# The last softmax chunk of the first message pass, twelve pairs, becomes one of eight and one of four

## What is computed

```python
h_src = h_all[edge_type, src]
scores = einsum(h_src, attn_src) + einsum(h_dst, attn_dst)
scores = where(scores > 0, scores, 0.2 * scores)
amax = maximum(segment_max(scores, dst), 0.0)
w = exp(scores - amax[dst])
denom = segment_sum(w, dst) + 1e-12
out = segment_sum(h_src * (w / denom[dst])[..., None], dst)
```

## Time and profile before

| what | us |
|---|---|
| three runs | 2943.80, 2944.15, 2945.18 |
| median | 2944.15 |
| span of the profiled execution | 2937.4 |
| median less span (what lies around it) | 6.75 |
| gathers of the first pass (POOL L1412), 392 of them | 355.7 to 848.4 |
| its first and last weighing (DVE L1643) | 407.3 and 891.8 |
| its last add (DVE L1657) ends | 894.4 |
| DVE, first instruction of the next stage | 895.5 |
| PE busy, DVE busy, ACT busy, POOL busy over the span | 78%, 48%, 36%, 46% |

### The profile page before, as it was taken

One profiled execution on the slowest core, in us unless ns is written; L12 is line 12 of the kernel. 1 busy time (PEld: TensorE's weight loads), 2 busy tenths in 40 slices (PEclk: granted clock), 3 DMA queues, 4 the chain that ended last, 5 costly groups with the idle time before them and its releaser, 6 DMA issues. The chain is left out here.

```text
span 2937.4 us, 42780 instructions
## 1 busy us (share of the span) xinstructions
PE 2285.9 (78%) x11338; PEld 1700.9 (58%) x11338; DVE 1402.4 (48%) x3454; ACT 1054.5 (36%) x2797; POOL 1365.4 (46%) x1426
## 2 busy tenths in 40 slices
PE   3899737767677988999994697876754998874996
PEld 3455324445455877888883465554543777663775
DVE  6665426667666231111115332242248666656677
ACT  2422224545442212332332443265411656441320
POOL 1122277777740051111110577777757777774300
PEclk8999958888878899999997898988775999997998
DMA  6256544444421024666763533343556444445001
GB/s 199 73 175 201 160 114 119 119 119 118 119 67 31 1 73 142 213 210 200 220 202 108 152 106 105 106 137 114 164 156 206 127 136 134 126 120 161 18 1 44
DMA packets 244439, 374.16 MB, mean 127 GB/s; under 512 B 66888, under 2 KB 179860, under 8 KB 244234
## 3 DMA queue, kind: packets, MB, share of 16 engines
q0 software_dynamic: 64624, 179.69, 21.4%
q1 hardware_dynamic: 132718, 140.75, 15.6%
q10 hardware_dynamic: 46892, 51.32, 5.3%
HBM read 301.77 MB, written 69.88 MB: 127 GB/s over the span
## 5 line engine op out<-in xcount | busy, mean ns | idle before, releaser
L2677 POOL DMA_INDIRECT cm_rows<-rows,e_bsrc x392 | 374.1, 954 | 202.0 <-issue 102.4
L1412 POOL DMA_INDIRECT at_rows<-values,e_brow x392 | 373.6, 953 | 139.8 <-issue 86.9
L1138 POOL DMA_INDIRECT store<-rows,e_bsrc x392 | 377.2, 962 | 119.5 <-issue 105.7
L1492 PE MATMUL at_part<-at_msg,store 128*128 128x265 f32 x880 | 272.4, 453 | 89.3 <-DVE at_msg L1643 46.5
L2813 PE MATMUL cm_part<-cm_rows,cm_one 128*128 x880 | 264.4, 443 | 89.2 <-SPq L2689 59.5
L1163 PE MATMUL banks<-ag_msg,ag_one 128*128 128x258 f32 x880 | 232.4, 401 | 74.5 <-issue 42.1
L2813 PEld LDWEIGHTS cm_part<-cm_rows,cm_one 128*128 128x128 f32 x880 | 179.5, 217 | 157.1 <-issue 133.9
L1492 PEld LDWEIGHTS at_part<-at_msg,store 128*128 128x128 f32 x880 | 176.3, 219 | 161.8 <-DVE at_msg L1643 71.8
L3028 DVE TENSOR_TENSOR store<-store,cm_part 128x256 f32 x220 | 92.1, 419 | 335.6 <-PE cm_part L2813 304.6
L1163 PEld LDWEIGHTS banks<-ag_msg,ag_one 128*128 128x128 f32 x880 | 166.1, 197 | 125.4 <-issue 57.2
L2114 POOL DMA_INDIRECT expert_out<-x_y,x_target x56 | 53.7, 960 | 370.5 <-DVE x_y L2217 363.2
(11 more groups left out here) (662 smaller groups left out, 3958.8 us busy)
## 6 DMA issues: line engine op xcount, KB each, us to landing
x_w<-in_L_ffn_W1p SPq DMA_DIRECT2D x32, 1024.0 KB, 5.1
x_w<-in_L_ffn_W2p SPq DMA_DIRECT2D x32, 1024.0 KB, 5.6
values<-p_hv ACTq DMA_DIRECT2D x25, 1088.0 KB, 4.9
p_brow<-local_row SPq DMA_DIRECT2D x44, 320.0 KB, 3.7
xn_acc<-low_row SPq DMA_DIRECT2D x28, 448.0 KB
expert_in<-z_z POOLq DMA_DIRECT2D x7, 1032.0 KB
je_y<-expert_out SPq DMA_DIRECT2D x25, 256.0 KB, 2.9
at_rows<-values,e_brow POOLq DMA_INDIRECT x392, 2.8
```

What stands on the lines that cost most here:

```text
L1138: pool.indirect_dma_start(rows[:, b % slots, k, :], None, table, bass.IndirectOffsetOnAxis(index[:, k, b:b + 1], 0)).then_inc(gathered[b % ...
L1412: pool.indirect_dma_start(rows[:, b % RING, k, :], None, table, bass.IndirectOffsetOnAxis(e.block_row[:, k, b:b + 1], 0)).then_inc(gathere ...
L1492: last = pe.matmul(part[:, bank["pair", n], 0:wide], one[:, n // U % 2, k, n % U, :], msg[:, n % 4, k, :], start=(k == 0), stop=(k == K2 - 1))
L2677: pool.indirect_dma_start(rows[:, b % SLOTS, k, :], None, table, bass.IndirectOffsetOnAxis(e.block_src[:, k, b:b + 1], 0)).then_inc(gather ...
```

## The change

The list of chunks ends in one of 8 pairs (208 to 215) and one of 4 (216 to 219). There are 15 chunks, and the first 13 are as before. Their score copies keep their places, 22 positions ahead. The copies of the two short chunks move: those of a chunk of m pairs stand at the m positions that end with its step 0, one at each, so pairs 208 to 215 at n = 195 to 202 and pairs 216 to 219 at n = 207 to 210. Step 0 of the chunk of eight stands at n = 202, where that of the chunk of twelve stood; step 0 of the chunk of four at n = 210.

```diff
-CHUNKS = [(lo, min(CH, G - lo)) for lo in range(0, G, CH)]
+SHORT = (8, 4)
+FULL = (G - sum(SHORT)) // CH
+assert FULL * CH + sum(SHORT) == G
+CHUNKS = [(q * CH, CH) for q in range(FULL)] + [(G - sum(SHORT[q:]), SHORT[q]) for q in range(len(SHORT))]
+CHUNK_OF = [(pc, j) for pc, (lo, m) in enumerate(CHUNKS) for j in range(m)]
...
+    fetch_at = {}
+    for pc, (lo, m) in enumerate(CHUNKS):
+        for j in range(m):
+            at = lo + j - FREE if pc < FULL else lo - LEAD - m + 1 + j
+            fetch_at.setdefault(max(at, -LEAD - 1), []).append(lo + j)
...
-                pc, j = n // CH, n % CH
+                pc, j = CHUNK_OF[n]
...
-            for n in range(FREE - LEAD):
+            for n in fetch_at[-LEAD - 1]:
                 fetch(n)
             for n in range(-LEAD, G):
                 if n >= 0 and n % U == 0 and n + U < G:
                     hots(n // U + 1)
-                if n + FREE < G:
-                    fetch(n + FREE)
+                for late in fetch_at.get(n, ()):
+                    fetch(late)
...
-                        dve.tensor_copy(tips[:, now, :, 0:1], tips[:, ago, :, CH:CH + 1])
-                        dve.tensor_copy(inc_h[:, :, 0:1], heads_of(car[:, ago], CH + 1)[:, :, CH:CH + 1]).then_inc(reset, 1)
+                        ended_at = CHUNKS[pc - 1][1]
+                        dve.tensor_copy(tips[:, now, :, 0:1], tips[:, ago, :, ended_at:ended_at + 1])
+                        dve.tensor_copy(inc_h[:, :, 0:1], heads_of(car[:, ago], ended_at + 1)[:, :, ended_at:ended_at + 1]).then_inc(reset, 1)
...
-                if n % CH == 0:
-                    pc = n // CH
+                if n in first:
+                    pc = first[n]
```

More of the change, by code:

```diff
@@ L971, in _ @@
             act.wait_ge(made, 1)
-            full, rest = G // CH, G % CH
-            for at, many, wide in ((0, full, CH), (full, 1, rest)):
-                of = slice(at * CH, at * CH + many * wide)
+            for at, many in ((0, FULL), *((FULL + q, 1) for q in range(len(SHORT)))):
+                lo_of, wide = CHUNKS[at]
+                of = slice(lo_of, lo_of + many * wide)
                 for dst, src, lo, hi in ((e.past, past, 1, wide + 1), (e.upon, upon, 0, wide - 1)):
```

## The result

The changed kernel takes 2966.46 us (median of four runs, 2964.5 to 2969.3), the kernel before 2944.66 in the same comparison: 1.0068 times as long, 95% interval 1.0056 to 1.0080. That is 16.5 to 23.6 us more; 2965.2 had been forecast, from 21.0 us more. A second measurement on another occasion gave 1.0065 (1.0047 to 1.0083).

The account below looks back on a forecast made before the run. After the gathers one chain through ACT, PE and DVE was taken to bound the kernel, no engine being full. Terms 14.85 + 5.7 + 0.4 = 21.0 us on 2944.15 gave 2965.2 us, 0.7% slower; range 2957.5 to 2972.5.

Parts of the forecast that it names:

- PE arrives 3.9 us after its data: Step 0 of the last chunk, before: PE begins at 857.40, ACT's last copies are done at 853.51; gathers do not hold it.
- slope of n = 202 later: Step 0 of the eight pairs: late copies and a slow turn put ACT's slope at 863.9 instead of 859.85, +4.05 us.
- PE idle before the two turns: Before the turns at n = 202 and n = 210, PE waits 4.2 and 4.5 us for late score copies.
- pair 209's product later: Behind step 0 at n = 202: +4.05 less 0.27 for the narrower chunk leaves everything from there on 3.8 us later.
- that product to the weighing of pair 210: Step 0 at n = 210: behind one-hot block and late copy, pair 210 is weighed at 896.25 instead of 881.40.
- weighing 210 to weighing 216: Steps 1 to 5 at n = 211 to 215: 12.9 us instead of 7.23, so +5.7.
- weighing 216 to the last add, more than before: Step 6 of the chunk of four: one more rescaling on DVE in the tail, +0.4 us.
- everything before pair 202 within a few tenths: Sign in the profile after: the stage ahead of pair 202 keeps its times within a few tenths of a us.
- The last copy decides: Faster rival at n = 202: step 0 follows pair 215's copy, second softmax hidden, stage ends 4.6 us earlier, 2939.5; chance 0.03.
- The second softmax is hidden: No-change rival in the last 20.1 us: new steps fall into DVE's 6.7 us idle, about 2945.7 us; chance 0.06.
- The copies are free: Slower rival at both short chunks: late copies cost nothing, only n = 210's slope waits for ACT; +14.6, 2958.8 us; chance 0.10.
- The clock stays low to the end: Slower rival: as forecast, but pairs 215 to 219 take 2.13 instead of 1.06 us on PE; +5.3, 2970.5 us; chance 0.15.

Follow-up runs that it names:

- before again: The kernel before, unedited, timed and profiled once more as a control: ratio 1.0000 (0.9990 to 1.0011), median 2945.27 us.
- changed again: The changed kernel, unedited, timed and profiled a second time as a control: ratio to before 1.0065 (1.0047 to 1.0083), median 2962.54 us.
- the one built so: The changed kernel with the score copies of both short chunks kept 22 positions ahead: ratio to before 1.0044 (1.0030 to 1.0057), median 2959.79 us.

## Why the prediction was right

**The bound.** "PE arrives 3.9 us after its data" held: nothing was gained from needing fewer copies for the first of the two chunks. The Trainium skill (Perfetto Trace Analysis, Optimizing Scalar/DVE Operations) says that breaking up instructions may let work complete sooner where ScalarE or VectorE cause bubbles (idle gaps) on other engines without being full. Here PE does wait for DVE, but DVE's part did not shrink with the piece. Pair 202 in the timeline of PE and its weighing in that of DVE, before:

```profile
862.91 2.13 PE L1492 MATMUL at_part<-at_msg,store 128*128 128x265 f32 x4 [4.15 <-DVE at_msg L1643]
```

```profile
862.18 0.68 DVE L1643 TENSOR_TENSOR at_msg<-at_rows,at_turn 128x528 f32<-128x528 f32 x1
```

and the weighing after the change:

```profile
867.11 0.67 DVE L1653 TENSOR_TENSOR at_msg<-at_rows,at_turn 128x528 f32<-128x528 f32 x1
```

From the slope to this weighing it is 2.33 us with twelve pairs (859.85 to 862.18) and 2.34 with eight (864.77 to 867.11). Eight pairs gave nothing back there, and the four cut off brought a chain of their own.

**The terms of the sum**, in the two pairs of profiles: before and changed, before again and changed again. Places of a step are counted from pair 201's product.

| term | forecast | first pair | second pair |
|---|---|---|---|
| slope of n = 202 later | 4.05 | 3.74 (6.03 - 2.29) | 3.98 (6.27 - 2.29) |
| PE idle before the two turns | 4.2, 4.5 | 4.30, 4.70 | 4.30, 4.70 |
| pair 209's product later | 3.8 | 1.98 (27.09 - 25.11) | 2.98 (26.53 - 23.55) |
| that product to the weighing of pair 210 | 9.75 | 9.60 | 9.71 |
| off: the same before (the weighing came first) | -1.27 | -1.27 | -0.68 |
| weighing 210 to weighing 216 | 12.9 | 12.68 | 12.68 |
| off: the same before | 7.23 | 7.23 | 7.23 |
| weighing 216 to the last add, more than before | 0.4 | 0.48 (6.24 - 5.76) | 1.58 (7.34 - 5.76) |
| sum | 20.9 | 18.8 | 20.4 |

The first two rows lead to the third and are not added; rows marked "off" are taken off. The prediction rounded its sum to 21.0. The late copies and both waits came as forecast. One term was too large in both pairs: that everything behind the first step 0 stays 3.8 late. In the first pair 3.2 of it is left when pair 207 begins (20.07 us behind pair 201's product before, 23.22 after), and pairs 207 to 209 take off the rest, with 3.84 us against 5.04. Pairs 204 and 205 too had taken 1.67 and 1.27 us after the change, and 2.14 and 2.10 before. With it goes the granted clock of this stretch, 0.68 after and 0.59 in this execution of before. In the second execution of before it was 0.78, and there 2.98 remain. So the size of this term is in part the executions' luck, and so is it that the tail came out 2.2 below the forecast in one pair and 0.6 in the other.

In the runs the change costs 16.5 to 23.6 us. The forecast of 21.0 and both tails, 18.8 and 20.4, lie in it; that the median of the runs is within 1.3 us of 2965.2 is closer than tails that repeat to 1 us can promise.

Two readings of the prediction need a word, though neither moved the forecast. It took the 6.75 us between median and span for what lies around the span, and in each timed run of before only 1.8 lie there (2.1 to 2.2 after the change); as the forecast adds its sum to the median, the error drops out. And the 1.50 us before 848.44, which it takes for a register load, has SP's signal as its end in the row. The same copy after the change, long behind the gathers, still has 1.37 ahead of it, so a register load of about that size it was. The sign "everything before pair 202 within a few tenths" failed by the 1.2 us named above, which stand ahead of the change; the others came: the copy of pair 215 at 862.69, pair 210 weighed at 895.43, the last add at 914.35.

**The rivals.** "The last copy decides" fell with PE's idle of 4.30 us behind a copy that now comes late, and with a tail that is longer. "The second softmax is hidden" fell with the 10.8 us. "The copies are free" was not this kernel, but gave the price of the one built so: 14.6 us forecast and 14.6 in the tail (15.5 against the second profile of before). "The clock stays low to the end" was not so in the first profile: pairs 215 to 218 took 4.12 us together, the full clock. In the second control it was so in part: the last five took 5.97 us (5.54 in the first profile), and DVE waited for one of their products:

```profile
910.71 0.43 DVE L1667 TENSOR_TENSOR store<-store,at_part 128x265 f32 x1 [1.35 <-PE at_part L1501]
```

There it is 7.34 us from weighing 216 to the last add instead of 6.24, so this execution lost 1.1 us of the 5.3 that the rival had.

## What to carry to other kernels

A piece of pipelined work that is cut in two pays its chain of hand-overs twice: here about 10 us for four pairs, with vector scans that take as long for four pairs (0.68 us on 32 partitions) as for twelve (0.69 on 96). Look first whether the consumer was waiting for the last input of the piece; here PE reached the step 3.9 us after it. On an in-order engine, see what each step stands behind in its own queue: 4.4 us blocks of bulk work ahead of 0.4 us links cost 11.0 us of tail in the changed kernel and 2.1 to 3.0 in the one before, and moving the bulk behind the links made even the old kernel 0.2% faster.

## What the runs showed that I had not expected

Work that nobody needs made a kernel a little faster: fourteen idle products on PE, in time in which it waited, brought the pair behind them from 2.13 to 1.16 us and the ratio to 0.9987 (0.9978 to 0.9996). But the granted clock of a stretch is not the program's alone: one kernel, twice profiled, had 0.59 and 0.78 in the same stretch, and 25.1 and 23.6 us for it. A comparison of two single profiles, as between before and the kernel with idle products, would have put all of that down to the edit. And a delay does not stay what it is: 1.8 us on ACT left 0.9 to 1.9 us at the end, and 3.7 to 4.0 left 1.4 to 3.5 at pair 209, by which profile of the change is set against which of before.
